# The second combine stage: fewer spare TensorE passes, and a wait ahead of the first store

## What is computed

```python
x = _layernorm(x + _L0_attn_ref(x, ...), axis=-1)
x = _layernorm(x + _L0_ffn_ref(x, ...), axis=-1)
return x
```

```python
xn = (x - mu) * jax.lax.rsqrt(var + LN_EPS) * ln_gamma + ln_beta
logits = jnp.clip(xf @ router_w.T, -CLAMP, CLAMP)
top_v, top_i = jax.lax.top_k(logits, K)
```

## Time and profile before

| | |
|---|---|
| median of three runs (lowest, highest) | 1537.68 us (1537.1, 1537.92) |
| the profiled execution's own time | 1541.09 us |
| its span | 1538.7 us |
| busy share of the span: TensorE, VectorE, GpSimd, ScalarE | 94%, 66%, 48%, 47% |
| the stage of this change in the span | 742.3 us (first transpose) to 772.4 us (routing begins) |
| TensorE's granted clock, mean over the span | 0.962 of full speed |

### The profile page before, as it was taken

The page is one execution under the profiler, slowest core; times in us unless marked ns, Lnnn a source line. Parts: engine busy times, 40 slices in busy tenths (PEclk is TensorE's granted clock), DMA queues, the critical chain, the costliest instruction groups (busy, mean ns, idle before and its releaser), DMA issues. The chain is left out here.

```text
span 1538.7 us, 35990 instructions
## 1 busy us (share of the span) xinstructions
PE 1451.6 (94%) x11738; PEld 1410.8 (92%) x11738; DVE 1011.0 (66%) x2768; ACT 727.8 (47%) x1734; POOL 745.5 (48%) x749
## 2 busy tenths in 40 slices
PE   8999993999999999999939999999999999999993
PEld 6888873999999999999939999999999999999992
DVE  5999986667667666667565556565656656566455
ACT  4677654455545545555543434343434433343333
POOL 3677651566666665665523444334434344433433
PEclk8999995999999999999959999999999999999996
DMA  7121223344344343352613232313232132421117
GB/s 258 42 69 44 65 73 82 90 97 101 50 96 94 49 103 74 68 130 38 206 37 110 48 94 32 115 28 110 31 109 38 28 110 31 113 34 28 29 24 229
DMA packets 64835, 123.41 MB, mean 80 GB/s; under 512 B 14336, under 2 KB 53120, under 8 KB 62080
## 3 DMA queue, kind: packets, MB, share of 16 engines
q0 software_dynamic: 36416, 46.58, 18.5%
q1 hardware_dynamic: 28352, 76.03, 13.7%
HBM read 79.66 MB, written 42.90 MB: 80 GB/s over the span
## 5 line engine op out<-in xcount | busy, mean ns | idle before, releaser
L1122 DVE TENSOR_TENSOR E_hraw<-E_sg,bank 128x256 f32<-128x256 f32 x320 | 134.6, 421 | 282.1 <-ACT E_sg L1051 282.1
L979 POOL DMA_INDIRECT acc<-ysb,IDX x160 | 258.5, 1615 | 126.6 <-ACT ysb L1083 60.6
L972 POOL DMA_INDIRECT E_mg<-meta,IDX x160 | 150.9, 943 | 338.4 <-DVE E_gate L1106 312.5
L1179 PE MATMUL bank<-E_xT,ws 128*128 128x256 f32 x960 | 271.4, 283 | 5.0 <-DVE E_xT L1097 5.0
L1180 PE MATMUL bank<-E_xT,ws 128*128 128x256 f32 x960 | 270.9, 282 | 0.0
L1181 PE MATMUL bank<-E_xT,ws 128*128 128x256 f32 x960 | 270.8, 282 | 0.0
L1133 DVE TENSOR_TENSOR E_hT<-E_hraw,E_hT 128x256 fp32r<-128x256 f32 x640 | 259.5, 416 | 0.0
L1051 ACT ACTIVATE E_sg<-bank 128x256 f32<-128x256 f32 x320 | 121.5, 384 | 255.5 <-PE bank L1181 253.7
L1129 DVE CAST E_hT<-E_hraw 128x256 fp32r<-128x256 f32 x640 | 203.9, 319 | 57.4 <-ACT E_hraw L1054 51.5
L1179 PEld LDWEIGHTS bank<-E_xT,ws 128*128 128x128 f32 x960 | 183.3, 191 | 5.8 <-issue 5.8
L1180 PEld LDWEIGHTS bank<-E_xT,ws 128*128 128x128 f32 x960 | 182.6, 190 | 0.0
(11 more groups left out here) (210 smaller groups left out, 3936.0 us busy)
## 6 DMA issues: line engine op xcount, KB each, us to landing
wraw<-in_w_ffn SPq DMA_DIRECT2D x8, 3072.0 KB, 10.6
wraw<-in_w_moe SPq DMA_DIRECT2D x8, 2048.0 KB, 8.0
X<-acc SPq DMA_DIRECT2D x15, 512.0 KB, 5.4
acc<-x SPq DMA_DIRECT2D x32, 128.0 KB, 1.7
xn<-xn SPq DMA_DIRECT2D x32, 128.0 KB, 1.7
acc<-X POOLq DMA_DIRECT2D x4, 1024.0 KB, 8.2
acc<-X SPq DMA_DIRECT2D x8, 512.0 KB, 4.5
out<-C_xo SPq DMA_DIRECT2D x8, 512.0 KB, 5.9
```

The lines of the kernel that those rows point to most:

```text
L972: nc.gpsimd.indirect_dma_start(out=mg[:, j, :], out_offset=None, in_=meta_dram, in_offset=at_slots(u, j)).then_inc(s_gm, 16)
L979: nc.gpsimd.indirect_dma_start(out=acc_dram, out_offset=at_slots(u, j), in_=ysb[:, j, :], in_offset=None, compute_op=ALU.add).then_inc(s_y ...
L1122: V.tensor_tensor(hraw[:, f % RING, :], sg[:, f % RING, :], bank[f % RING][:, UW:2 * UW], ALU.mult).then_inc(s_hm, 1)
L1179: nc.tensor.matmul(out, wh, mh, start=first, stop=False)
```

## The change

Two edits, both in class `Between`. In `tensor`, the three spare passes ahead of tile 8 go, and of the one in each turn of the loop those with `n` from 0 to 9 stay: 10 spare passes are left of 38. In `sync`, SP waits for the last of its eight loads before its first store.

```diff
         for i in range(HEAD, len(SPANS)):
             t = slice(*SPANS[i])
             sp.dma_start(self.X[:, t, :], by_partition(self.io["acc1"])[:, t, :]).then_inc(self.s_ldx[i], 16)
+        sp.wait_ge(self.s_ldx[-1], 16)
         self.store(sp, range(GROUPS - LATE))
...
         for n in range(NT + 3):
-            if n == HEAD * G:
-                keep_busy(nc, self.bank[7], self.ws0, 3)
             if n < NT:
                 turn(n)
-            keep_busy(nc, self.bank[7], self.ws0, 1)
+            if n < HEAD * G + 2:
+                keep_busy(nc, self.bank[7], self.ws0, 1)
             if n >= 3:
                 logits(n - 3)
```

## The result

The changed kernel takes 1545.67 us (median of six runs, 1543.06 to 1548.0), the kernel before in the same comparison 1537.68 us (1536.21 to 1538.08). The ratio is 1.005, with a 95% interval of 1.0039 to 1.0061: **8 us slower**. The forecast was 1532.2; the time lies 0.9 us above the upper end of the range, and it is rival 1 that came true.

What follows compares the result with a forecast made beforehand. TensorE's pace of 0.849 us a tile was taken to bound the stage; 19 tiles without a 0.29 us pass save 5.5 us, the wait zero: 1537.68 - 5.5 = 1532.2 us, range 1531.2 to 1544.8.

Steps and rivals of the forecast that it cites:

- rival 1: TensorE's clock falls to half without the spare passes, tiles take 1.15 us, kernel slower at 1544.2 us; chance 0.33.
- It stands on TensorE keeping its full clock: Condition of the main forecast, 1532.2 us at chance 0.48: granted clock 1.00 from 749 to 766.
- worth nothing as time: The three spare passes ahead of tile 8 stand in a load wait, so removing them was counted as no gain.
- The row that I took as relief: Evidence against rival 1: earlier in the span TensorE was idle for 1.12 us and the clock stayed at 1.00.
- The pace at full clock: TensorE's tiles 12 to 31 go from 0.849 to 0.56 us each, 0.29 a pass, 5.5 us in all.
- if the parts add up: Sizing one spare pass on TensorE from start distances: 0.46 + 0.68 - 0.849 = 0.29 us, lower bound 0.23.
- the forecast's own range: Range of the full-clock forecast for the whole kernel, without the rivals: 1531.1 to 1533.3 us.
- once down it would stay down: Part of rival 1: a busy TensorE does not regain its clock, as from 786 to 796 at 0.50.
- Rival 2: TensorE's clock falls late or in some executions, gain and loss cancel, around 1537.7 us; chance 0.13.
- Who could take over: Check whether GpSimd or loads would limit the stage at TensorE's 0.56 us a tile; both were found ahead.
- rival 3: Full clock, but a loop of VectorE, ScalarE and copies holds tiles at 0.65 us; 1533.9 us, chance 0.06.
- The added wait: SP's first store waits for the last load, near 758 to 759; gain counted as zero, ends 0 and 0.5 us.

Runs made afterwards that it cites:

- e2: The kernel before without the three spare passes ahead of tile 8, all others kept: 1558.02 us, ratio 1.0127.
- e1: The changed kernel with the three spare passes ahead of tile 8 put back: 1538.85 us, ratio 0.9997 to the kernel before.
- e8: The kernel before with two spare passes instead of one at each of n = 12 to 31: ratio 1.0029.
- e3: The kernel before with only SP's wait ahead of the first store added, no spare pass removed: 1537.92 us, ratio 0.9996.
- e4: The changed kernel without SP's added wait, spare passes still removed: 1545.67 us, ratio 1.0041 to the kernel before.
- e10: The kernel before with every second spare pass from tile 10 on, plus SP's wait ahead of the first store: ratio 0.9971.
- e6: The kernel before with every spare pass from n = 12 on 256 columns wide instead of 512: ratio 0.9994.
- e7: The kernel before, keeping from tile 10 on only the spare passes of n divisible by four: ratio 1.0003.
- e9: The kernel before, keeping from tile 10 on only the spare passes of even n, a repeat run: ratio 0.9970.

## Why the prediction was wrong

**The step that failed** is the sentence "It stands on TensorE keeping its full clock", and the 0.48 that it got against rival 1's 0.33. The forecast had 1.00 from 749 to 766 and tiles 0.56 us apart; the clock fell to 0.50 at 745.7, right behind the wait for tile 8, and tiles were 1.17 us apart. The forecast counted the three passes there as "worth nothing as time", since they stood in a wait. That was true of their time and false of their work: taking them alone cost 20 us (e2). Putting them back gave the median back (e1). The row that I took as relief, 1.12 us of idle time without a fall, had passes of 264 columns ahead of it and of 136 behind, and was shorter; it was no price for 1.48 us. The other idle time I had, 1.4 us ahead of a fall, was the nearer one. The wait for tile 8 was also taken too short, at 1.2 us. Beyond that, the full clock was not safe even with the wait filled (e1). Where an operation is costed at nothing because it stands in a wait, what it does to the state of its engine must be costed too.

**The pace at full clock** was mis-sized in one term. A pass costs 0.23 us (e8), the lower bound, not 0.29; a tile without it is 0.62 us (e1), not 0.56. The step "if the parts add up" failed: they miss by 0.06 us. One reading fits: without the pass TensorE's weight loads are busy for 8.80 of 8.80 us (e1), where they were for 15.43 of 16.20 with it, so they may set the 0.62; no run shows it by itself. With the right size the gain would have been 19 x 0.23 = 4.4 us, or 1533.3, the upper end of the forecast's own range. The Trainium skill's figure for such a pass by itself ("TensorE: Matmul & The Clock Gate", Back-to-back issue gap) is 216 ns. The 0.23 us measured here is some 15 ns above it, and nearer to it than my 0.29.

**Rival 1** was right in its mechanism and its sizes: 1.15 us a tile taken, 1.17 measured; 0.8 us behind tile 31 taken, 0.8 measured; "once down it would stay down", which e2 shows most plainly. There is some luck in the pace: it was added up from 0.87 for the logits and 0.34 for the transposes, which are 0.71 and 0.46 from start to start (766.17, 766.63, 766.88 in the trace of the change), and the errors cancel. It was 1544.2 against 1545.67 because the fall came at tile 8 and not at tile 12: tiles 8 to 12 took 750.46 - 745.26 = 5.2 us where they had taken 3.5, another 1.7. That is also why the range ended 0.9 us short. The Trainium skill's rule that spoke against the change ("Perfetto Trace Analysis", Matmul Optimizations) asks for matmuls back to back. The granted clock of 0.50 from 745.7 on, behind the wait, agrees with it. In e1 the clock fell with TensorE back to back.

**Rival 2**, a clock that falls late or in some executions, describes not the change but the kernel with the three passes back (e1, median 1538.85 against 1538.07).

**Who could take over**: nobody did in e1, where 8.8 us ran at 0.62 us a tile, though VectorE was busy for 8.65 of them. Its groups start 2.29 us apart there:

```profile
753.97 1.37 DVE L1323 BATCH_NORM_STATS2 C_st<-X 128x6 f32<-128x256 f32 x4
...
756.26 1.36 DVE L1323 BATCH_NORM_STATS2 C_st<-X 128x6 f32<-128x256 f32 x4
```

The forecast had 2.03, and four of its tiles were 2.24. So at the forecast's pace VectorE would have been about at the limit; the mechanism of rival 3 was nearer than its 0.06 says.

**The added wait** was costed at 0 to 0.5 us, and no worth of it is measured, alone (e3), with the change (e4) and with every second pass (e10). The stores went out as the last load landed, and the routing phase covered them, as said.

## What to carry to other kernels

Filler matmuls on TensorE are priced by what they keep up, not by what they take: before any is removed, remove it alone and look at the granted clock of the stretch behind, since three instructions in a wait decided 20 us here. A stretch that is 100% busy with narrow passes may still be too thin, and thinning filler out step by step, with the spread of single executions and not the median as the sign of danger, found some 3 us. Where a DMA is kept from colliding with another, ask first whether anyone waits for either.

## What the hardware showed that I had not expected

The clock can fall with TensorE busy up to the fall: in e1 at 759.2, behind 8.8 us of passes back to back, transposes of 128 columns and logits of 8. And a TensorE that the profile calls fully busy need not get it back: in e2 it was busy for 33 us of 33 at 0.50, with a pass of 512 columns in each tile. In the changed kernel it came back at 820.8, amid the second expert phase's matmuls of 256 columns, back to back.

By their times and mean clocks, executions of the same program differ in whether they lose the clock (e6, e7), and in e1 perhaps in when. Even the kernel before is not quite safe: one of its 24 executions beside e9, of 88 in all, took 1560.03 us with a mean granted clock of 0.953, the picture of e2, where the others beside it had 0.961 to 0.966. The ratios above leave it out. Whether that one fell at tile 8 as well has no trace to show it.
